# Winograd products with other signs, column sums from two blocks, and one block summed by transfers

## The chip, the core and the metric

The kernel runs on one core of a Trainium2 chip. The metric is the device time in microseconds of one execution.

## What is computed

```python
# for each of 128 samples b, x[b] is 64 x 1024
h     = gelu(gelu(cond @ W0 + b0) @ W1 + b1)
att   = softmax(h @ W2 + b2)                       # 128 x 8
agg_w = einsum('bk,koi->boi', att, weight)         # 64 x 64 for each sample
y     = agg_w[b] @ x[b] + (att @ bias_k)[b]        # mixes the 64 rows of a sample
logits, h = y @ W_router.T, y @ A.T                # 8 experts, rank 16, the top 2 of a softmax
out   = x + y @ W_base.T + b_base + 2 * (h * combine) @ B
```

All in fp32, 8192 rows of 1024 numbers.

## The kernel before

The two matmuls that take y's 1024 columns are one: A, W_router and W_base lie side by side in a matrix "wide" of 1024 x 1160 (128 columns for A, 8 for the router, 1024 for the base). Mixing a sample's rows and multiplying by "wide" commute, so the kernel first computes z = x @ wide, and then mixes: each pair of samples is a tile of 128 rows, multiplied by a block-diagonal 128 x 128 matrix ("mix", from agg_w). The bias agg_b of a row passes through "wide" as agg_b times the column sums of "wide"; these are computed once, by matmuls with a matrix of ones, into `col_sum` (lines 437 to 446).

**Splitting.** TensorE multiplies in fp32r. Each operand is a high part (a cast on ScalarE, `x_high`, `split_weight`) and a low part (the rest, by a subtraction on VectorE, `x_low`, `split_weight`, lines 912 and 1009). A product is high·high + high·low + low·high, three matmuls of 128 x 128 by 128 x 290 columns each (lines 416, 418, 420).

**Seven products.** Two tiles make a unit, 32 units in all. A unit's x is a 2 x 2 matrix of blocks (A11, A12 for the first tile, A21, A22 for the second; each 128 rows by 512), and "wide" is one too (B11, B12, B21, B22; each 512 x 580, split into 4 chunks of rows). From unit 1 on, Winograd's form of Strassen's scheme takes seven block products in place of eight; each is 24 matmuls. It needs sums of x's blocks (S1 to S4, made on VectorE for every unit, lines 915 to 928) and of the blocks of "wide" (T1 to T4, made once, line 1018, and split once, lines 722 and 1009). Unit 0 takes the plain eight products, while "wide" is still coming in; the T blocks are made beside it.

**What sets the order.** All five engines have their instructions written out by hand, in order, with semaphore waits. The stretch that matters is the end of unit 0 and unit 1. TensorE (lines 561 to 584): products A11·B12 and A12·B22 for Z12, the matmul that makes `agg_b` (line 567), the column sums of B11 and B21, the products A21·B12 and A22·B22 for Z22, with the column sums of B12 and of B22 between and after them, then mixing of tile 0 (`mixed`). The column sums and the matmul of agg_b use PSUM banks that the products and mixing use too: the A21·B12 product waits for VectorE's two copies of agg_b (line 1053), and a new set of column sums for ScalarE's copy of the last (line 733). ScalarE's order is in lines 776 to 796, VectorE's in lines 1041 to 1072, its unit 1 in lines 1074 to 1119. In unit 1 TensorE waits for the low parts of T2, T3 and T4 (lines 601, 610, 621), T1 being ready long before.

Staging: `w_stage` has two slots, B11's and B21's; T1, T2 and later T3 are made in B11's slot and T4 in B21's. B12 and B22 lie in `b12_sb` and `b22_sb`, whose bytes other buffers of the later work take over. `w_hi` and `w_lo` have six slots for seven blocks, B12's slot being given to another block after unit 0.

POOL makes the low part of "mix" (line 882) and adds x to the biases by an accumulating transfer (`add_x`, line 889): VectorE writes the biases into `x_sb` (`put_biases`, line 1002), the transfer adds x, and VectorE adds the result from PSUM (`result`, lines 995 and 997). SP issues all other loads and stores.

## Time and profile before

| | |
|---|---|
| median of 3 runs | 954.32 us (954.03 to 954.56) |
| the profiled execution | 954.3 us, its span 952.6 us |
| TensorE busy | 945.1 us, 99% of the span |
| VectorE, ScalarE, POOL busy | 695.5, 332.8, 89.1 us |
| share of the chain that ended last | TensorE 97%, DMA 1%, VectorE 1% |
| HBM | 75.37 MB read, 35.65 MB written, 117 GB/s over the span |

The span is the time from the first to the last instruction in the profile; the execution's own time is 1.7 us longer. Times in the timelines are from the start of the span. Matmuls are pipelined, so one that is printed as 0.30 us long starts 0.13 us after the one before it.

### The profile page before, as it was taken

Reading aid. Unit: us, or ns where it says so; the run is one execution under the profiler, and the core shown is the slowest. Engines: PE = TensorE matmul, PEld = TensorE weight load, DVE = VectorE, ACT = ScalarE, POOL = GpSimd, SP = SyncE. Lnnn points to the kernel's source line nnn. Section 1 sums busy time; section 2 is a strip of 40 time slices with the busy share of each in tenths; the row PEclk is TensorE's granted clock in tenths of the full one; section 3 lists DMA queues with packets and bytes.
Section 4 is the critical chain, followed back from the end, with each engine's and each line's share of the span. In section 5 each row is a group of like instructions: output and inputs, shape, how many; then the busy total and the mean of one; then the engine's idle time right before and its main releaser. Section 6 shows DMA issues by size and latency. Waiting matters only on the chain.

```text
span 952.6 us, 18810 instructions
## 1 busy us (share of the span) xinstructions
PE 945.1 (99%) x6745; PEld 940.2 (99%) x6745; DVE 695.5 (73%) x1554; ACT 332.8 (35%) x671; POOL 89.1 (9%) x134
## 2 busy tenths in 40 slices
PE   9999999999999999999999999999999999999997
PEld 8999999999999999999999999999999999999997
DVE  4889776768776768777777777777777677767686
ACT  5653332333332333332333333333333333323431
POOL 0011010101010100100100100010101010101010
...
GB/s 304 140 75 132 110 119 132 92 132 91 111 115 133 90 134 91 111 113 130 94 133 92 112 113 119 105 118 105 114 113 109 115 108 104 120 118 104 120 90 111
DMA packets 35233, 111.33 MB, mean 117 GB/s; under 512 B 13040, under 2 KB 13424, under 8 KB 30864
## 3 DMA queue, kind: packets, MB, share of 16 engines
...
q10 hardware_dynamic: 288, 1.19, 0.4%
...
q14 instruction: 6, 0.05, 0.0%
HBM read 75.37 MB, written 35.65 MB: 117 GB/s over the span
## 4 chain that ended last, share of the span: by engine, by line
PE 97%; DMA 1%; DVE 1%; issue 0%; ACT 0%; DVEq 0%; ACTq 0%
PE ps L416 25%; PE ps L420 25%; PE ps L418 25%; PE ps L476 9%; PE ps L452 4%; PE ps L450 4%; PE ps L454 4%; DMA w_stage<-in_wide 1%; PE ps L499 1%; PE ps L442 0%; PE ps L443 0%; PE ps L502 0%; PE ps L513 0%; DVE sum L931 0%; DVE x_sb L1220 0%
## 5 line engine op out<-in xcount | busy, mean ns | idle before, releaser
L416 PE MATMUL ps<-w_hi,x_hi 128*128 128x290 f32 x1544 | 460.3, 298 | 0.3 <-DVE sum L931 0.3
L418 PE MATMUL ps<-w_lo,x_hi 128*128 128x290 f32 x1544 | 457.7, 296 | 0.0
L420 PE MATMUL ps<-w_hi,x_lo 128*128 128x290 f32 x1544 | 456.9, 296 | 0.0
L416 PEld LDWEIGHTS ps<-w_hi,x_hi 128*128 128x128 f32 x1544 | 291.5, 189 | 2.5 <-issue 1.5
L420 PEld LDWEIGHTS ps<-w_hi,x_lo 128*128 128x128 f32 x1544 | 291.3, 189 | 0.0
L418 PEld LDWEIGHTS ps<-w_lo,x_hi 128*128 128x128 f32 x1544 | 291.2, 189 | 0.0
L684 ACT CAST x_hi<-xT_sb 128x512 fp32r<-128x512 f32 x186 | 115.6, 621 | 190.9 <-DVE xT_sb L928 163.4
L912 DVE TENSOR_TENSOR x_lo<-xT_sb,x_hi 128x512 fp32r<-128x512 f32 x186 | 127.4, 686 | 34.3 <-ACT x_hi L684 34.3
L889 POOL DMA_DIRECT2D x_sb<-in_x x64 | 56.4, 881 | 512.0 <-DVE x_sb L1002 512.0
L988 DVE TENSOR_TENSOR hwT_lo<-ps,hwT_hi 128x128 fp32r<-128x128 f32 x64 | 18.7, 291 | 97.7 <-ACT hwT_hi L696 96.9
L699 ACT COPY sum<-ps 128x580 f32<-128x580 f32 x96 | 61.9, 645 | 62.9 <-PE ps L420 62.1
L1002 DVE SCALAR_TENSOR_TENSOR x_sb<-col_sum,agg_b,bias_out 128x1024 f32<-128x1024 f32 x64 | 81.8, 1279 | 1.0 <-ACT col_sum L733 1.0
L931 DVE TENSOR_TENSOR sum<-ps,sum 128x580 f32<-128x580 f32 x92 | 69.6, 757 | 12.7 <-PE ps L420 12.6
L416 PE MATMUL ps<-t_hi,x_hi 128*128 128x290 f32 x248 | 76.4, 308 | 0.0
L420 PE MATMUL ps<-t_hi,x_lo 128*128 128x290 f32 x248 | 74.0, 298 | 0.0
L418 PE MATMUL ps<-t_lo,x_hi 128*128 128x290 f32 x248 | 73.4, 296 | 0.0
L707 ACT CAST z_hi<-sum 128x580 fp32r<-128x580 f32 x31 | 21.0, 678 | 148.8 <-DVE sum L931 148.8
L450 PE MATMUL ps<-z_hi,mix_hi 128*128 128x384 f32 x189 | 64.2, 339 | 0.7 <-DVE x_sb L997 0.7
L452 PE MATMUL ps<-z_hi,mix_lo 128*128 128x384 f32 x189 | 64.2, 340 | 0.0
L882 POOL TENSOR_TENSOR mix_lo<-mix,mix_hi 128x128 fp32r<-128x128 f32 x64 | 32.3, 506 | 340.1 <-ACT mix_hi L688 340.1
L454 PE MATMUL ps<-z_lo,mix_hi 128*128 128x384 f32 x189 | 63.5, 336 | 0.0
L997 DVE TENSOR_TENSOR x_sb<-ps,x_sb 128x776 f32<-128x776 f32 x62 | 59.2, 955 | 0.0
...
## 6 DMA issues: line engine op xcount, KB each, us to landing
x_sb<-in_x POOLq DMA_DIRECT2D x64, 512.0 KB, 5.4
result<-x_sb SPq DMA_DIRECT2D x63, 512.0 KB, 2.8
...
b_sb<-in_wide SPq DMA_DIRECT2D x2, 1160.0 KB, 14.7
agg_w_rows<-agg_w SPq DMA_DIRECT2D x1, 2048.0 KB, 7.5
...
```

What stands on the lines that cost most here:

```text
L416: nc.tensor.matmul(dst, x_hi[:, s, rows], high[:, c, cols], start=first, stop=False, skip_group_check=True)
L418: nc.tensor.matmul(dst, x_hi[:, s, rows], low[:, c, cols], start=False, stop=False, skip_group_check=True)
L420: mm = nc.tensor.matmul(dst, x_lo[:, s, rows], high[:, c, cols], start=False, stop=last, skip_group_check=True)
L450: nc.tensor.matmul(dst, mix_hi[:, side, :], high[:, columns(k)], start=start, stop=False, skip_group_check=True)
L452: nc.tensor.matmul(dst, mix_lo[:, side, :], high[:, columns(k)], start=False, stop=False, skip_group_check=True)
L454: return nc.tensor.matmul(dst, mix_hi[:, side, :], low[:, columns(k)], start=False, stop=True, skip_group_check=True)
L476: mm = nc.tensor.matmul(ps[:, banks[k], at], stat[:], mov[:, res], start=False, stop=True, skip_group_check=True)
L684: nc.scalar.copy(x_hi[:, SLOT[name], :], raw(name)).then_inc(x_hi_done, 1)
L699: nc.scalar.copy(dst[:], acc(first)).then_inc(done, 1)
L912: nc.vector.tensor_tensor(x_lo[:, SLOT[name], :], raw(name), x_hi[:, SLOT[name], :].bitcast(F32), ALU.subtract).then_inc(x_lo_done, 1)
L931: nc.vector.tensor_tensor(dst[:], acc(first), dst[:], ALU.add).then_inc(done, 1)
L1002: nc.vector.scalar_tensor_tensor(x_sb[:, side, :], col_sum[:, AR:WIDE], agg_b[:, bass.ds(tile_no(u, side), 1)], bias_out[:], ALU.mult, ALU.add
```

## The change

- The signs of S1, S2 and S3 are turned, and T1 to T4 follow: T1 = B12 - B11, T2 = T1 + B22, T3 = B12 + B22, T4 = B21 - T2. S1 goes with T1, S2 with T2, S3 with T3 and A22 with T4, as before.
- T3 + T4 = B11 + B21, and T3 is B12 + B22. So the column sums of T4 and of T3 suffice: T3's are the right half, and the left half is the sum of both, one more VectorE instruction. Two blocks are summed by TensorE instead of four.
- T3 is not made on VectorE: two accumulating transfers, issued by POOL, add B22 from HBM onto B12 in `b12_sb`.
- T4 and T3 are split in unit 0, T2 and T1 in unit 1 (before: T1 and T2 in unit 0, T3 and T4 in unit 1). T1 has the separate pair of buffers that T3 had.
- On VectorE, T1, T2 and T4 are made one after the other, ahead of the copies of agg_b. The low part of B goes from before the first biases into unit 1, and the biases of tile 1 go behind the low part of T1.
- SP loads the small table ahead of the rest of unit 0's x.

```diff
@@ -45,8 +45,9 @@
-B11, B21, T1, B22, T2, T4, T3 = range(7)
-B12 = T4
+B11, B21, T3, B22, T2, T4, T1 = range(7)
+B12 = T3
@@ -165,8 +166,8 @@
-        t3_hi = sb("t3_hi", [P, CHUNKS, HALF], F32R)
-        t3_lo = sb("t3_lo", [P, CHUNKS, HALF], F32R)
+        t1_hi = sb("t1_hi", [P, CHUNKS, HALF], F32R)
+        t1_lo = sb("t1_lo", [P, CHUNKS, HALF], F32R)
@@ -255,21 +258,22 @@
-        SPLIT_AT = {"B11": 4, "B21": 6, "B12": 7, "B22": 8, "T1": 9, "T2": 10, "T3": 11, "T4": 12}
+        SPLIT_AT = {"B11": 4, "B21": 6, "B12": 7, "B22": 8, "T4": 9, "T3": 10, "T2": 11, "T1": 12}
-        T_AT = {"T1": 1, "T2": 2, "T4": 3, "T3": 4}
+        T_AT = {"T1": 1, "T2": 2, "T4": 3}
-            return (t3_hi, t3_lo) if w == T3 else (w_hi[:, w, :, :], w_lo[:, w, :, :])
+            return (t1_hi, t1_lo) if w == T1 else (w_hi[:, w, :, :], w_lo[:, w, :, :])
-        b11_stage = t_stage = chunked(w_stage[:, 0, :])
+        b11_stage = t1_stage = chunked(w_stage[:, 0, :])
-        b12_stage = chunked(b12_sb[:])
-        b22_stage = chunked(b22_sb[:])
+        b12_stage = t3_stage = chunked(b12_sb[:])
+        b22_stage = t2_stage = chunked(b22_sb[:])
@@ -355,9 +359,9 @@
             sp.dma_start(xT_sb[:, 0, :], xT_units[0][:, 0:XBLOCK]).then_inc(first_xT_in[0], 16)
+            sp.dma_start(small_sb[:], small).then_inc(small_in, 16)
             sp.dma_start(xT_sb[:, 1:4, :].rearrange("p b n -> p (b n)"), xT_units[0][:, XBLOCK:]
-            sp.dma_start(small_sb[:], small).then_inc(small_in, 16)
@@ -434,16 +438,14 @@
                     mm = product_part(bank, name, part, start)
                 mm.then_inc(product_mm, 1)
-            def column_sums(bank, w, start=False, stop=False):
+            def column_sums(bank, w):
                 high, low = weight_parts(w)
                 for part in range(2):
                     dst, cols = ps[:, bank + part, 0:PART], slice(part * PART, (part + 1) * PART)
                     for c in range(CHUNKS):
-                        nc.tensor.matmul(dst, ones_r[:], high[:, c, cols], start=start and c == 0, stop=False)
-                        mm = nc.tensor.matmul(dst, ones_r[:], low[:, c, cols], start=False,
-                                              stop=stop and c == CHUNKS - 1)
-                if stop:
-                    mm.then_inc(col_mm, 1)
+                        nc.tensor.matmul(dst, ones_r[:], high[:, c, cols], start=c == 0, stop=False)
+                        mm = nc.tensor.matmul(dst, ones_r[:], low[:, c, cols], start=False, stop=c == CHUNKS - 1)
+                mm.then_inc(col_mm, 1)
             def mixed(side, k, bank=None, high=z_hi, low=z_lo, start=True):
                 dst = ps[:, O_BANK + k if bank is None else bank, 0:width(k)]
@@ -565,15 +567,15 @@
             first_product(b, "A12", B22, False)
             pe.wait_ge(agg_done, 2 * GROUPS)
             chain(ps[:, O_BANK, 0:BATCH], mix_w_sb[0:KERNELS, GROUP_COLS:MIX_COLS], attT[0:KERNELS, :], agg_b_mm)
-            pe.wait_ge(ones_done, 1)
-            column_sums(O_BANK + 2, B11, start=True)
-            column_sums(O_BANK + 2, B21, stop=True)
             pe.wait_ge(agg_b_done, 2)
             first_product(O_BANK, "A21", B12, True)
+            first_product(O_BANK, "A22", B22, False)
+            pe.wait_ge(ones_done, 1)
+            pe.wait_ge(w_lo_done, SPLIT_AT["T4"])
+            column_sums(O_BANK + 2, T4)
             pe.wait_ge(col_sum_done, 1)
-            column_sums(O_BANK + 2, B12, start=True)
-            first_product(O_BANK, "A22", B22, False)
-            column_sums(O_BANK + 2, B22, stop=True)
+            pe.wait_ge(w_lo_done, SPLIT_AT["T3"])
+            column_sums(O_BANK + 2, T3)
             pe.wait_ge(z22_summed, 1)
             pe.wait_ge(mix_lo_done, 1)
             pe.wait_ge(z11_lo_done, 1)
@@ -604,10 +606,10 @@
+                if first:
+                    pe.wait_ge(w_lo_done, SPLIT_AT["T1"])
-                if first:
-                    pe.wait_ge(w_lo_done, SPLIT_AT["T3"])
@@ -617,8 +619,6 @@
-                if first:
-                    pe.wait_ge(w_lo_done, SPLIT_AT["T4"])
@@ -776,24 +776,26 @@
             aggregated(0)
             z11_high(0)
             aggregated(1)
-            act.wait_ge(t_made, T_AT["T1"])
-            split_weight(T1, t_stage)
             act.wait_ge(product_mm, FIRST_PRODUCT["A12", B22])
             save(sum2, b, z12_summed)
             act.wait_ge(xT_in, 16)
             x_high("A11")
-            column_sum(0)
+            act.wait_ge(t_made, T_AT["T4"])
+            split_weight(T4, t4_stage)
+            z12_high(0)
             for side in range(2):
                 mix_high(0, side)
-            z12_high(0)
-            act.wait_ge(t_made, T_AT["T2"])
-            split_weight(T2, t_stage)
+            act.wait_ge(t3_in, 32)
+            act.wait_ge(product_mm, FIRST_PRODUCT["A21", B12])
+            split_weight(T3, t3_stage)
+            act.wait_ge(product_mm, FIRST_PRODUCT["A22", B22])
+            save(sum3, O_BANK, z22_summed)
             x_high("A12")
+            column_sum(0)
+            split_weight(T2, t2_stage)
+            column_sum(1)
             act.wait_ge(bT_in, 16)
             nc.scalar.copy(b_hi[:], bT_stage).then_inc(b_hi_done, 1)
-            act.wait_ge(product_mm, FIRST_PRODUCT["A22", B22])
-            save(sum3, O_BANK, z22_summed)
-            column_sum(1)
             def unit(u, par, first=False):
                 a, b = accumulators(par)
@@ -809,8 +811,8 @@
-                    act.wait_ge(t_made, T_AT["T3"])
-                    split_weight(T3, t_stage)
+                    act.wait_ge(w_lo_done, SPLIT_AT["T3"])
+                    split_weight(T1, t1_stage)
@@ -819,8 +821,6 @@
-                if first:
-                    split_weight(T4, t4_stage)
@@ -888,6 +888,13 @@
                 pool.wait_ge(biased, t + 1)
                 pool.dma_start(x_sb[:, side, :], x_tiles[t], accum_op=ALU.add).then_inc(x_in[side], 16)
+
+            pool.wait_ge(b12_in, 16)
+            pool.wait_ge(w_lo_done, SPLIT_AT["B12"])
+            pool.wait_ge(t_made, T_AT["T1"])
+            for js in HALVES:
+                cols = slice(js.start * HALF, js.stop * HALF)
+                pool.dma_start(b12_sb[:, cols], wide_blocks[3][:, cols], accum_op=ALU.add).then_inc(t3_in, 16)
             for side in range(2):
                 mix_low(0, side)
             add_x(0, 0)
@@ -913,15 +920,15 @@
-                nc.vector.tensor_tensor(raw("S1"), raw("A21"), raw("A22"), ALU.add).then_inc(s_made, 1)
+                nc.vector.tensor_tensor(raw("S1"), raw("A21"), raw("A22"), ALU.subtract).then_inc(s_made, 1)
-                nc.vector.tensor_tensor(raw("S3"), raw("A11"), raw("A21"), ALU.subtract).then_inc(s_made, 1)
+                nc.vector.tensor_tensor(raw("S3"), raw("A21"), raw("A11"), ALU.subtract).then_inc(s_made, 1)
-                nc.vector.tensor_tensor(raw("S2"), raw("S1"), raw("A11"), ALU.subtract).then_inc(s_made, 1)
+                nc.vector.tensor_tensor(raw("S2"), raw("A11"), raw("S1"), ALU.subtract).then_inc(s_made, 1)
@@ -1014,8 +1021,8 @@
                 nc.vector.tensor_tensor(x_lo[:, FIRST_SLOT[name], :], xT_sb[:, RAW[name], :],
                                         x_hi[:, FIRST_SLOT[name], :].bitcast(F32), ALU.subtract).then_inc(x_lo_done, 1)
-            def make_t(dst, left, right):
-                nc.vector.tensor_tensor(dst, left, right, ALU.subtract).then_inc(t_made, 1)
+            def make_t(dst, left, right, op=ALU.subtract):
+                nc.vector.tensor_tensor(dst, left, right, op).then_inc(t_made, 1)
             nc.vector.memset(att[:], 0.0).then_inc(att_step, 1)
             first_x_low("A11")
@@ -1041,34 +1048,34 @@
             split_weight(B12, SPLIT_AT["B12"], b12_stage)
             split_weight(B22, SPLIT_AT["B22"], b22_stage)
             dve.wait_ge(w_lo_done, SPLIT_AT["B11"])
-            make_t(t_stage, b12_stage, b11_stage)
+            make_t(t1_stage, b12_stage, b11_stage)
+            dve.wait_ge(w_lo_done, SPLIT_AT["B22"])
+            dve.wait_ge(t_made, T_AT["T1"])
+            make_t(t2_stage, t1_stage, b22_stage, ALU.add)
+            dve.wait_ge(t_made, T_AT["T2"])
+            make_t(t4_stage, b2_stage, t2_stage)
             z11_low(0)
-            dve.wait_ge(xT_in, 16)
-            make_s1(1)
-            make_s3(1)
             dve.wait_ge(agg_b_mm, 1)
             for par in range(PAIR):
                 rows = slice(par * CH, (par + 1) * CH)
                 of_tiles = ps[rows, O_BANK, 0:BATCH].rearrange("p (t par) -> p t par", par=PAIR)[:, :, par]
                 nc.vector.tensor_copy(agg_b[rows, :], of_tiles).then_inc(agg_b_done, 1)
-            split_weight(T1, SPLIT_AT["T1"], t_stage)
+            dve.wait_ge(xT_in, 16)
+            make_s1(1)
+            make_s3(1)
+            split_weight(T4, SPLIT_AT["T4"], t4_stage)
+            split_weight(T3, SPLIT_AT["T3"], t3_stage)
+            z12_low(0)
             x_low(1, "A11")
-            dve.wait_ge(w_lo_done, SPLIT_AT["T1"])
-            dve.wait_ge(t_made, T_AT["T1"])
-            make_t(t_stage, b22_stage, t_stage)
-            z12_low(0)
-            dve.wait_ge(t_made, T_AT["T2"])
-            make_t(t4_stage, b2_stage, t_stage)
-            split_weight(T2, SPLIT_AT["T2"], t_stage)
             x_low(1, "A12")
             dve.wait_ge(x_lo_done, splits(1, "A11"))
             make_s2(1)
-            dve.wait_ge(b_hi_done, 1)
-            nc.vector.tensor_tensor(b_lo[:], bT_stage, b_hi[:].bitcast(F32), ALU.subtract).then_inc(b_lo_done, 1)
+            dve.wait_ge(col_sum_done, 2)
+            nc.vector.tensor_tensor(col_sum[:, 0:HALF], col_sum[:, 0:HALF], col_sum[:, HALF:WIDE], ALU.add
+                                    ).then_inc(col_left_done, 1)
             dve.wait_ge(bias_out_in, 16)
             dve.wait_ge(agg_w_out, 16)
-            dve.wait_ge(col_sum_done, 2)
-            dve.wait_ge(b_lo_done, 1)
+            dve.wait_ge(col_left_done, 1)
             put_biases(0, 0)
             def unit_1():
@@ -1077,21 +1084,23 @@
                 z21_low(0, b)
                 route(0, 0)
                 x_low(1, "S2")
+                dve.wait_ge(b_hi_done, 1)
+                nc.vector.tensor_tensor(b_lo[:], bT_stage, b_hi[:].bitcast(F32), ALU.subtract).then_inc(b_lo_done, 1)
+                hwT_low(0, 0)
+                split_weight(T2, SPLIT_AT["T2"], t2_stage)
                 z22_low(0)
-                hwT_low(0, 0)
-                x_low(1, "S1")
-                put_biases(0, 1)
-                dve.wait_ge(w_lo_done, SPLIT_AT["T2"])
-                dve.wait_ge(t_made, T_AT["T4"])
-                make_t(t_stage, b22_stage, b12_stage)
                 dve.wait_ge(p1_saved, 1)
                 dve.wait_ge(product_mm, products(1, "A12"))
                 add_acc(sum1, b, z11_summed)
                 result(0, 0)
+                x_low(1, "S1")
+                dve.wait_ge(w_lo_done, SPLIT_AT["T2"])
+                split_weight(T1, SPLIT_AT["T1"], t1_stage)
+                dve.wait_ge(b_lo_done, 1)
+                put_biases(0, 1)
                 x_low(1, "S3")
                 dve.wait_ge(x_lo_done, splits(1, "A12"))
                 make_s4(1)
-                split_weight(T3, SPLIT_AT["T3"], t_stage)
                 route(0, 1)
                 x_low(1, "S4")
                 x_low(1, "A22")
@@ -1100,7 +1109,6 @@
-                split_weight(T4, SPLIT_AT["T4"], t4_stage)
```

VectorE at the end of unit 0: the rows after the low parts of B12 and B22, before (`w_stage` holds T1, then T2 and T4; `b_sb` is b12_sb or b22_sb).

```order
L1018 TENSOR_TENSOR w_stage<-b_sb,w_stage 128x2320 [waits w_lo_done]
L935 TENSOR_TENSOR z_lo<-sum,z_hi 128x580 [waits z11_hi_done]
L916 TENSOR_TENSOR s_sb<-xT_sb 128x512 [waits xT_in]
L920 TENSOR_TENSOR xT_sb<-xT_sb 128x512 [waits s_made]
L1053 COPY agg_b<-ps 64x64 [waits agg_b_mm]
L1053 COPY agg_b<-ps 64x64
L1009 TENSOR_TENSOR w_lo<-w_stage,w_hi 128x2320 [waits w_hi_done]
```

The same place with the change.

```order
L1025 TENSOR_TENSOR w_stage<-b_sb,w_stage 128x2320 [waits w_lo_done]
L1025 TENSOR_TENSOR b_sb<-w_stage,b_sb 128x2320 [waits t_made,w_lo_done]
L1025 TENSOR_TENSOR w_stage<-w_stage,b_sb 128x2320 [waits t_made]
L942 TENSOR_TENSOR z_lo<-sum,z_hi 128x580 [waits z11_hi_done]
L1062 COPY agg_b<-ps 64x64 [waits agg_b_mm]
L1062 COPY agg_b<-ps 64x64
L923 TENSOR_TENSOR s_sb<-xT_sb 128x512 [waits xT_in]
L927 TENSOR_TENSOR xT_sb<-xT_sb 128x512 [waits s_made]
L1016 TENSOR_TENSOR w_lo<-w_stage,w_hi 128x2320 [waits w_hi_done]
L1016 TENSOR_TENSOR w_lo<-b_sb,w_hi 128x2320 [waits w_hi_done]
```

Three makes of a T stand ahead of the two copies of agg_b, where one stood; the two sums of x's blocks went behind them.

TensorE at the matmul of agg_b, before (the two rows ahead of it end A12·B22; the rows behind it begin the column sums).

```order
L418 MATMUL ps<-w_lo,x_hi 128x290
L420 MATMUL ps<-w_hi,x_lo 128x290
L502 MATMUL ps<-attT,mix_w_sb 128x128 [waits agg_done]
L442 MATMUL ps<-w_hi,ones_r 128x290 [waits ones_done]
L443 MATMUL ps<-w_lo,ones_r 128x290
```

The same place with the change.

```order
L422 MATMUL ps<-w_lo,x_hi 128x290
L424 MATMUL ps<-w_hi,x_lo 128x290
L504 MATMUL ps<-attT,mix_w_sb 128x128 [waits agg_done]
L420 MATMUL ps<-w_hi,x_hi 128x290 [waits agg_b_done]
L422 MATMUL ps<-w_lo,x_hi 128x290
```

The product that waits for the copies of agg_b comes right behind the matmul that makes it.

VectorE in unit 1, from the first low part of an S block to the make of S4, with the change.

```order
L919 TENSOR_TENSOR x_lo<-xT_sb,x_hi 128x512 [waits x_hi_done]
L1088 TENSOR_TENSOR b_lo<-x_sb,b_hi 128x1024 [waits b_hi_done]
L995 TENSOR_TENSOR hwT_lo<-ps,hwT_hi 128x128 [waits hwT_hi_done]
L1016 TENSOR_TENSOR w_lo<-b_sb,w_hi 128x2320 [waits w_hi_done]
L957 TENSOR_TENSOR z_lo<-sum,z_hi 128x580 [waits z22_hi_done]
L938 TENSOR_TENSOR sum<-ps,sum 128x580 [waits product_mm,p1_saved]
L1002 TENSOR_TENSOR x_sb<-ps,x_sb 128x248 [waits out_mm,x_in_a]
L1004 TENSOR_TENSOR x_sb<-ps,x_sb 128x776
L919 TENSOR_TENSOR x_lo<-s_sb,x_hi 128x512 [waits x_hi_done]
L1016 TENSOR_TENSOR t_lo<-w_stage,t_hi 128x2320 [waits w_hi_done,w_lo_done]
L1009 SCALAR_TENSOR_TENSOR x_sb<-col_sum,agg_b,bias_out 128x1024 [waits b_lo_done]
```

Two splits of a T (rows L1016, of T2 and T1) and b_lo now stand between the low part of S2 and the biases of tile 1, where the make of T3 stood alone.

## Rows read from the trace of the kernel before

**Rows 1.** The page, busy time of the engines
```profile
PE 945.1 (99%) x6745; PEld 940.2 (99%) x6745; DVE 695.5 (73%) x1554; ACT 332.8 (35%) x671; POOL 89.1 (9%) x134
```

**Rows 2.** TensorE's waits, whole span: who waited for whom, total, times, longest, us
```profile
PE ps L513 <- ACT w_hi L722: 0.9, 1, 0.9
```

**Rows 3.** TensorE's timeline: start us, duration us, engine, line, operation, tiles
```profile
33.73 0.40 PE L442 MATMUL ps<-w_hi,ones_r 128*128 128x290 f32 x1
33.97 0.30 PE L443 MATMUL ps<-w_lo,ones_r 128*128 128x290 f32 x1
...
38.01 0.30 PE L443 MATMUL ps<-w_lo,ones_r 128*128 128x290 f32 x1
...
48.86 0.33 PE L450 MATMUL ps<-z_hi,mix_hi 128*128 128x384 f32 x1
```

**Rows 4.** VectorE's timeline, end of unit 0
```profile
25.21 2.58 DVE L1009 TENSOR_TENSOR w_lo<-b_sb,w_hi 128x2320 fp32r<-128x2320 f32 x1 [0.82 <-ACT w_hi L722]
27.70 2.57 DVE L1018 TENSOR_TENSOR w_stage<-b_sb,w_stage 128x2320 f32<-128x2320 f32 x1
30.19 0.76 DVE L935 TENSOR_TENSOR z_lo<-sum,z_hi 128x580 fp32r<-128x580 f32 x1
...
33.84 0.48 DVE L1053 COPY agg_b<-ps 64x64 f32<-64x64 f32 x2 [1.57 <-PE ps L502]
```

**Rows 5.** SP's and ScalarE's timelines, and the landing times of b12_sb and b22_sb
```profile
6.36 0.45 SPq L369 DMA_DIRECT2D b_sb<-in_wide  x1
...
23.04 2.14 ACT L722 CAST w_hi<-b_sb 128x2320 fp32r<-128x2320 f32 x1
...
38.34 0.65 ACT L733 COPY col_sum<-ps 128x580 f32<-128x580 f32 x1 [3.19 <-PE ps L443]
...
DMA to landing us min/median/max: 12.7/14.7/16.6
```

**Rows 6.** Timelines of VectorE, ScalarE and TensorE, 47 to 65 us
```profile
47.69 1.22 DVE L1067 TENSOR_TENSOR b_lo<-x_sb,b_hi 128x1024 fp32r<-128x1024 f32 x1 [0.30 <-ACT b_hi L793]
49.91 1.28 DVE L1002 SCALAR_TENSOR_TENSOR x_sb<-col_sum,agg_b,bias_out 128x1024 f32<-128x1024 f32 x1 [1.00 <-ACT col_sum L733]
51.32 0.76 DVE L945 TENSOR_TENSOR z_lo<-ps,z_hi 128x580 fp32r<-128x580 f32 x1
...
53.87 0.68 DVE L912 TENSOR_TENSOR x_lo<-xT_sb,x_hi 128x512 fp32r<-128x512 f32 x1
...
61.35 0.95 DVE L997 TENSOR_TENSOR x_sb<-ps,x_sb 128x776 f32<-128x776 f32 x1
...
64.06 0.64 ACT L699 COPY sum<-ps 128x580 f32<-128x580 f32 x1
...
58.39 0.30 PE L416 MATMUL ps<-w_hi,x_hi 128*128 128x290 f32 x1
...
62.45 0.41 PE L450 MATMUL ps<-z_hi,mix_hi 128*128 128x384 f32 x1 [0.68 <-DVE x_sb L997]
...
64.11 0.29 PE L416 MATMUL ps<-w_hi,x_hi 128*128 128x290 f32 x1
```

**Rows 7.** DMA: 83 to 89 us; issues of 125 to 140 us, then whole span
```profile
83.00:89.00 6.00, 5.97 (x44) 5.74 (x43) 5.20 (x19) 1.72 (x5) 1.22 (x2) 1.00 1.00 178
...
x_sb<-in_x POOLq DMA_DIRECT2D x1, 512.0 KB, 5.4
result<-x_sb SPq DMA_DIRECT2D x1, 512.0 KB, 5.3
...
result<-x_sb SPq DMA_DIRECT2D x63, 512.0 KB, 2.8
agg_w_rows<-agg_w SPq DMA_DIRECT2D x1, 2048.0 KB, 7.5
```

**Rows 8.** Warm-up matmuls by stretch: us, busy and (count) for matmul, then load, clock, DMA
```profile
4.00:7.00 3.00, 3.00 (x16) 3.00 (x15) 1.00 0.94 323
7.00:8.50 1.50, 1.50 (x15) 1.50 (x13) 1.00 0.98 407
```

2 lines of the change are left out of this document (added).

## The prediction

> **What bounds the kernel now.** I read the page's busy line first, then TensorE's waits, then the timelines of TensorE, VectorE and ScalarE from 20 to 80 us, and last the transfers. TensorE is busy in 945.1 of 952.6 us [rows 1]; its waits are few, and the largest after its first matmul is 0.9 us, for a cast of B11 [rows 2]. So a matmul taken out of TensorE's stream is time taken out of the span, if everything TensorE then waits for is ready earlier by as much. The reader is to see in the timelines that, after the first loads, VectorE is nearly as full as TensorE up to 80 us: it makes and splits the seven weight blocks there. The profiled execution took 954.3 us beside a median of 954.32, so I add to 954.3.
>
> A rule of reading that I use throughout: on VectorE an operation starts about 0.09 us before the printed end of the one before it, if it does not depend on it (25.21 to 27.70 is 2.49 for a row of 2.58 [rows 4]). One that needs the other's result starts about 0.04 us after it.
>
> **1. Column sums, removed.** Before, B11, B21, B12 and B22 are summed, 16 matmuls each. Now T4 and T3 alone: 32 fewer. The spacing is (38.01 - 33.97) / 30 = 0.1347 us [rows 3]. 32 x 0.1347 = **-4.31 us**, all on TensorE's path.
>
> **2. agg_b, a new wait.** The column sums of B11 and B21 stood between the matmul that makes agg_b (it ends at about 33.8) and the product A21·B12, which writes the same PSUM bank and so must wait for VectorE's two copies of agg_b. Those sums ran from 33.73 to 38.1 [rows 3] and the copies at 33.84 to 34.32 [rows 4]: hidden. Now the product comes at once, and on VectorE three makes of a T (T1, T2, T4) stand ahead of the copies instead of one. Worked out from rows 4: T1 27.70 to 30.27; T2 needs T1, 30.31 to 32.88; T4 needs T2, 32.92 to 35.49; the low part of Z11 starts at 35.41, and the copies at 36.08, ending at 36.56. TensorE goes on at about 36.66 instead of 33.73: **+2.93 us**. Queued behind this wait are both remaining products of unit 0, both column sums and all of unit 1. The start of the chain is fixed by a transfer: B22 lands at 6.36 + 16.6 = 22.96, its cast starts at 23.04 [rows 5], its low part at 25.21. The wait could be 0.2 either side of this.
>
> **3. T4's sums to T3's sums, a new wait.** Both use one pair of banks. Before, a product lay between a pair of sums and the next. Now T3's sums wait for ScalarE's copy of T4's. From rows 3 and 5: the last sum of a pair started at 38.01, the copy ran from 38.34 to 38.99, so TensorE can go on at 39.04, where it would have at 38.14: **+0.90 us**, and 0.10 for one more restart (the first matmul after a wait takes 0.24 instead of 0.13, 33.73 to 33.97 [rows 3]).
>
> So the first mixing matmul of unit 0, at 48.86 before [rows 3], comes 4.31 - 2.93 - 0.90 - 0.10 = **0.38 us earlier**, at 48.48. The second copy of column sums is then at 48.7 to 49.35, with the cast of T2 done on ScalarE before it.
>
> **4. T3 by transfers.** POOL waits for T1 (30.27) and issues two accumulating transfers of 580 KB at about 30.6. Two of 512 KB kept the engines full for 6 us at 178 GB/s [rows 7]; 1.19 MB at that rate is 6.7 us, starting 1.5 us after the issue: landed at about 39.3. ScalarE may not cast T3 before A21·B12 has been multiplied (w_hi's slot), at about 40.2, and TensorE needs T3's low part at 46.3, which allows the cast to start as late as 41.5 (2.14 + 2.57 + small change). So the transfer is hidden, with 2.2 us in hand; I take **0**. What shares the engines is the 2,048 KB store of agg_w from 35.3 on [rows 7]. Beside an add, a store of 512 KB took 5.3 us instead of 2.8, while the add kept its 5.4 [rows 7]: the store pays, and nobody waits for agg_w before 49. Bounds: 0, and +2 if the two queues shared evenly (below). The Trainium skill's page "DMA: Bandwidth & Descriptors", section "Queues, rings and completion order", says that an engine goes round-robin between the queues it has work for, a packet at a time; by that T3 would be slowed as well, and the sum would be up to 2 us higher. The rows speak for the add keeping its pace.
>
> **5. Unit 1, where VectorE sets the pace.** VectorE now adds the two halves' sums first (580 columns, 0.76) and then makes the first biases: 49.55 + 0.76 + 0.04 = 50.35, instead of 49.91 [rows 6]. From there to the low part of S2 it took 3.96, of which 0.22 was a wait before Z21 (51.32) that is over now: 54.09. Then low S2 0.60, b_lo 1.13, hwT_lo 0.21, and the low part of T2 from 56.05 to **58.61**. TensorE wants T2 at 58.39 - 0.38 = 58.01 [rows 6]: it waits 0.70 with the latency of 0.1. Low Z22 0.67, Z11's sum 0.67, result 1.20 (before, this result was what mixing waited for, 0.68 [rows 6]; now it is out at 61.2, in time), low S1 0.60, and T1's low part ends at **64.24**. TensorE, from 58.71: S2 24 x 0.1347 + 0.1 to 62.04, mixing 1.60 to 63.64, then T1: another 0.70, to 64.34. Biases 1.20, low S3 0.60, S4 made by 66.65; ScalarE casts it and then saves U2, done at **67.86** instead of 64.70 [rows 6]; TensorE, ready at 67.67, starts S3 at 67.91. Before, it started S3 at 64.11 + 3.23 = 67.34 [rows 6]. So unit 1 turns the lead of 0.38 into a lag of 0.57, with the restart **0.67 us**. Bounds for this part: each of those three instants may be off by 0.3.
>
> **6. The rest.** From unit 2 on a subtraction stands where an addition stood, of the same size and place: 0. No T is split late in unit 1 any more (two splits and a make fewer there, one split and b_lo more), so nothing is carried into unit 2. The table "small" is loaded ahead of 768 KB of x: B11's second half may land sooner, which is worth 0 to 0.9 us at TensorE's wait [rows 2]. But whatever is gained is lost at step 2, because there TensorE waits for a chain that hangs on B22's landing, whose place in the queue has not moved: 0 in the sum, and a wait of up to 3.8 us instead of 2.9.
>
> **Sum:** -4.31 + 2.93 + 0.90 + 0.10 + 1.05 (unit 1: from -0.38 to +0.67) = +0.67. Forecast **955.0 us**, no change: about 1.9 us (0.2%) is what a measurement can tell.
>
> **Rivals.** (a) *The clock falls in the new gap: slower.* Since its first matmul TensorE has never stood still for more than 0.9 us [rows 2]. After standing idle, the warm-up passed 16 matmuls in 3 us from 4 to 7, and 15 in 1.5 us from 7 to 8.5, at a clock column of 1.00 in both [rows 8]: a half-speed stretch of some 5.9 us (1.1 to 7.0) that the column does not show. If an idle gap of 2.9 to 3.8 us brings that back, at the lower of the two levels (1.2 and 2.4 GHz), TensorE loses half of up to 5.9 us: +1.7 to +2.9, giving 956.7 to 957.9. It decides from the point at which the gap is long enough, and the trace has none to tell. The Trainium skill, "TensorE: Matmul & The Clock Gate", Part 1, has the throttled state as the default to which an idle engine returns; by that rule this is the case, if the gap is long enough. Chance 0.25. (b) *T3 lands late: slower.* If from 36 us both queues get half, the last 2.8 us of T3 take 5.6 or, with the store's larger pieces, 7.4: 41.7 to 43.4, so 0.2 to 1.9 after the limit of 41.5: up to 956.9. Against it: rows 7. Chance 0.08. (c) *The wait at agg_b is short and unit 1 does not wait: faster.* Then only 0.9 is given back: 954.3 - 4.3 + 1.0 = 951.0. It would need the three makes to take 3.2 us less; rows 4 give 2.57 each. Chance 0.05. (d) *The start's 0.9 us counts after all,* as B22 lands sooner too: 954.1. Chance 0.07, and still no change.
>
> **How the numbers follow.** The forecast itself 0.55, at 954.2 to 956.0. Faster by over 0.2% only by (c), with room for something not seen: 0.07. Slower by over 0.2% (over 956.2): (a), and half of (b), 0.28. No change: 0.65. The range goes from (d) to (a): 953.6 to 958.0.
>
> **What would show it.** Right: TensorE waits about 2.9 us (up to 3.8) before its first product after the agg_b matmul, released by VectorE's copy; 0.9 us between the two runs of column sums, released by ScalarE; 0.7 us each before S2 and S1 in unit 1, released by splits; and no wait in mixing at 62. Wrong: the copies of agg_b at 34 us; T3's cast starting later than 41.5; matmuls 0.25 us apart after the gap; or unit 2 starting at another lag than 0.67.

## The result, and the profile after

| | before | changed |
|---|---|---|
| median, in the same session | 954.4 us (12 runs, 954.03 to 954.77) | 956.85 us (12 runs, 956.49 to 957.41) |
| the profiled execution, its span | 954.3, 952.6 us | 956.55, 954.7 us |
| mean granted clock over the span | 1.000 | 0.998 |

The ratio is 1.0025, with an interval of 1.0018 to 1.0033: the changed kernel is 2.4 us slower. That lies inside the predicted range (953.6 to 958.0), but the forecast itself, 955.0 and no change, was 1.85 us too low, and it was the wrong case: slower by more than 0.2%, to which the prediction had given 0.28.

The page, busy time of the engines, of the changed kernel:

```profile
PE 942.5 (99%) x6713; PEld 936.8 (98%) x6713; DVE 693.7 (73%) x1554; ACT 332.3 (35%) x671; POOL 88.1 (9%) x136
```

Against [rows 1] there are 32 matmuls fewer, as the diff says. At the 0.1347 us of step 1 the busy time should be 4.3 us less, and it is 2.6 less. So there is more than new waits: some matmuls became longer. The waits of TensorE, in the columns of [rows 2]:

```profile
PE ps L420 <- DVE agg_b L1062: 3.3, 1, 3.3
...
PE ps L446 <- DVE w_lo L1016: 1.1, 1, 1.1
PE ps L420 <- DVE t_lo L1016: 0.6, 1, 0.6
PE ps L420 <- issue: 0.6, 1, 0.6
...
PE ps L515 <- ACT w_hi L722: 0.3, 1, 0.3
```

The first is the predicted wait for agg_b. The second was predicted as a wait for ScalarE's copy of the column sums, but it is VectorE's split of T3 that ends it. The next two are T1 and T2 in unit 1 (that of T2 is put down to "issue"). The last was 0.9 in [rows 2]. TensorE's timeline gives the places (start, duration, then what ended the idle time before it):

```profile
32.44 0.48 PE L504 MATMUL ps<-attT,mix_w_sb 8*128 8x128 f32 x2
...
36.21 0.40 PE L420 MATMUL ps<-w_hi,x_hi 128*128 128x290 f32 x1 [3.29 <-DVE agg_b L1062]
...
44.24 0.29 PE L446 MATMUL ps<-w_hi,ones_r 128*128 128x290 f32 x1
...
46.24 0.29 PE L447 MATMUL ps<-w_lo,ones_r 128*128 128x290 f32 x1
47.59 0.38 PE L446 MATMUL ps<-w_hi,ones_r 128*128 128x290 f32 x1 [1.06 <-DVE w_lo L1016]
...
60.14 0.37 PE L420 MATMUL ps<-w_hi,x_hi 128*128 128x290 f32 x1 [0.59 <-issue]
...
65.81 0.37 PE L420 MATMUL ps<-t_hi,x_hi 128*128 128x290 f32 x1 [0.64 <-DVE t_lo L1016]
...
69.31 0.40 PE L420 MATMUL ps<-w_hi,x_hi 128*128 128x290 f32 x1
```

Between 36.21 and 44.24 there are 48 matmuls. At the usual spacing they take 6.5 us, and they took 8.03. The stretches of 1 us (the stretch, its length, busy time and number of instructions of PE, PEld, DVE, ACT and POOL) show why (the last three columns are the granted clock, the DMA share and GB/s):

```profile
36.00:37.00 1.00, 0.79 (x5) 0.80 (x6) 0.94 (x3) 1.00 (x1) 0.00 (x0) 0.93 0.91 146
37.00:38.00 1.00, 1.00 (x6) 1.00 (x5) 1.00 (x2) 0.83 (x2) 0.00 (x0) 0.50 0.97 175
38.00:39.00 1.00, 1.00 (x6) 1.00 (x6) 1.00 (x1) 0.00 (x0) 0.00 (x0) 0.50 0.99 192
39.00:40.00 1.00, 1.00 (x6) 1.00 (x6) 1.00 (x1) 0.00 (x0) 0.00 (x0) 0.50 0.48 96
40.00:41.00 1.00, 1.00 (x8) 1.00 (x8) 0.09 (x1) 0.00 (x0) 0.00 (x0) 0.86 0.37 32
41.00:42.00 1.00, 1.00 (x10) 1.00 (x9) 0.00 (x0) 0.00 (x0) 0.00 (x0) 1.00 1.21 499
```

TensorE stood for 3.29 us and started again at 36.21, and from 36.9 (0.93 is a mean over the stretch) to 40.3 the granted clock was 0.50, the 1.2 GHz level: 3.4 us. This is rival (a). ScalarE's and VectorE's timelines show that T3 was late as well, as in rival (b):

```profile
42.12 0.69 ACT L688 CAST mix_hi<-mix 128x128 fp32r<-128x128 f32 x2 [4.29 <-DMA mix<-agg_w]
42.71 2.13 ACT L722 CAST w_hi<-b_sb 128x2320 fp32r<-128x2320 f32 x1
...
44.87 2.58 DVE L1016 TENSOR_TENSOR w_lo<-b_sb,w_hi 128x2320 fp32r<-128x2320 f32 x1 [4.79 <-ACT w_hi L722]
```

The cast of T3 began at 42.71, not at 40.2, and later than the limit of 41.5 that step 4 gives. And the transfers behind it (issue, landing; first SyncE's, then by group):

```profile
31.27 7.54 SPq L351 DMA_DIRECT2D mix<-agg_w  x4
...
b_sb<-in_wide POOLq DMA_DIRECT2D x2, 580.0 KB, 9.5
...
mix<-agg_w SPq DMA_DIRECT2D x4, 16.0 KB, 8.0
```

T3's two halves took 8.3 and 10.8 us instead of the 8.2 of step 4 (1.5 and 6.7), so that the second landed at 42.1. The four loads of 16 KB for the first two mixing matrices took 8.0 to land, and 7.54 to be issued. In the profile before, the same four were issued at 32.15 in 3.08 us and landed in 2.7.

The twelve executions are not all like the profiled one. Seven have a mean clock of 0.998 over the span and a median of 956.70 us; five have 0.995 or 0.996 and a median of 957.09. What a lower mean clock looks like is shown by the profiles of runs 3, 5 and 9 below.

So there are two suspects, and they stand in parallel: the clock makes A21·B12 and A22·B22 end 1.5 us late, and T3's low part, wanted right behind them, is late too. The experiments had to part them.

### The profile page after: what moved, and what is told of

The parts are those of the page before. It is cut to its first block, busy times and chain, and to the rows that moved or that the text cites. A ratio compares the mean times of both kernels' runs of the same rounds, so it can differ in the third digit from the quotient of the medians.

```text
span 954.7 us, 18751 instructions
## 1 busy us (share of the span) xinstructions
PE 942.5 (99%) x6713; PEld 936.8 (98%) x6713; DVE 693.7 (73%) x1554; ACT 332.3 (35%) x671; POOL 88.1 (9%) x136
## 3 DMA queue, kind: packets, MB, share of 16 engines
q10 hardware_dynamic: 288, 1.19, 0.4%
## 4 chain that ended last, share of the span: by engine, by line
PE 95%; DVE 2%; DMA 2%; ACT 1%; SPq 0%; issue 0%; DVEq 0%; ACTq 0%
PE ps L420 25%; PE ps L424 24%; PE ps L422 24%; PE ps L478 9%; PE ps L454 3%; PE ps L452 3%; PE ps L456 3%; DMA w_stage<-in_wide 1%; DMA mix<-agg_w 1%; PE ps L501 1%; SPq L351 0%; ACT w_hi L722 0%; PE ps L504 0%; DVE w_lo L1016 0%; DVE t_lo L1016 0%
## 5 line engine op out<-in xcount | busy, mean ns | idle before, releaser
L420 PE MATMUL ps<-t_hi,x_hi 128*128 128x290 f32 x248 | 73.7, 297 | 0.6 <-DVE t_lo L1016 0.6
L882 POOL TENSOR_TENSOR mix_lo<-mix,mix_hi 128x128 fp32r<-128x128 f32 x64 | 29.7, 465 | 308.3 <-ACT mix_hi L688 308.3
```

The source lines that it names most:

```text
L420: nc.tensor.matmul(dst, x_hi[:, s, rows], high[:, c, cols], start=first, stop=False, skip_group_check=True)
```

## Experiments

Times are medians, with the kernel before run beside them on the same chip: 954.36 for runs 1 to 4, 954.44 for runs 5 to 7 and 11, 954.37 for runs 8 to 10 and 12. The rows of a run come from one execution, the profiled one.

**1. The gap taken away.**

```diff
+            (the two copies of agg_b)
             dve.wait_ge(t_made, T_AT["T2"])
             make_t(t4_stage, b2_stage, t2_stage)
...
-            (the two copies of agg_b)
```

> The copies of agg_b ahead of T4's make on VectorE. Theory M (what sets the time is T3's low part, at 47.4 us, because ScalarE's cast of T3 stands behind the casts of mix, whose loads land 8.0 us after their issue beside the transfers that add B22): TensorE waits 0.6 instead of 3.3 us for agg_b, the clock does not fall, and TensorE then waits about 2.5 us longer for T3's low part; the time stays within 0.3 us of the change's 956.85. Theory C (the wait for agg_b and the fallen clock are on the path): 2.7 + 1.6 us less, minus some 0.7 that T4 is later: 953.3.

Measured: 958.62 us, ratio 1.0045 (1.0031 to 1.0059), slower than the changed kernel. A row of TensorE's timeline and one stretch, in its last three columns the granted clock, the DMA share and GB/s:

```profile
47.89 0.58 PE L446 MATMUL ps<-w_hi,ones_r 128*128 128x290 f32 x1 [4.57 <-DVE w_lo L1016]
...
48.00:49.00 1.00, 1.00 (x5) 1.00 (x6) 1.00 (x3) 0.76 (x1) 0.00 (x0) 0.50 0.47 70
```

The gap at agg_b shrank to 0.57 and the clock stayed at 1.00 behind it. T4's sums started at 40.93. But T3's sums could not start before 47.89: the same gap, with the same fall of the clock behind it, now fell between the two runs of column sums. Here T3 sets the end of unit 0, not agg_b. Theory M had the waits right, but the time lies 1.8 us over its 956.85: it had no fall of the clock behind the second gap.

**2. T3 cast before the mixing matrices.**

```diff
             act.wait_ge(t3_in, 32)
-            for side in range(2):
-                mix_high(0, side)
             split_weight(T3, t3_stage)
+            for side in range(2):
+                mix_high(0, side)
```

> ScalarE casts T3 ahead of the two casts of mix. Theory M with C (both end at nearly the same instant): T3's cast starts at 40.9, when A21*B12 is through, its low part ends at 45.7, and TensorE is now held by the copy of T4's sums, at 47.26 instead of 47.59: 956.5. Theory M alone (the clock's fall costs nothing anywhere): T3 1.8 us sooner gives up to 1.8 us: 955.1.

Measured: 956.83 us, 1.0024 (1.0015 to 1.0033), as the changed kernel.

```profile
42.14 2.13 ACT L722 CAST w_hi<-b_sb 128x2320 fp32r<-128x2320 f32 x1 [4.17 <-DMA b_sb<-in_wide]
...
47.41 0.40 PE L446 MATMUL ps<-w_hi,ones_r 128*128 128x290 f32 x1 [0.73 <-ACT col_sum L733]
```

The order on ScalarE was not the cause: now the transfer itself ends the wait, at 42.14, and only 0.57 of lateness goes. T3's sums then wait for ScalarE's copy, 0.18 sooner than before, and the time does not move, since the clock fell in the gap as before. Together with run 4 below: either cause alone is enough for almost all of the delay.

**3. Both edits.** 

> Both edits: copies of agg_b ahead of T4's make, and T3's cast ahead of the casts of mix. Theory M with C: no long gap, no fall of the clock; TensorE waits 0.7 for T4's low part and starts T3's sums at about 45.1 instead of 47.59, 2.5 us less: 954.4, though either edit alone gives at most 0.3. If the two costs simply add: the sum of the gains of the two edits alone.

Measured: 957.94 us, 1.0035 (1.0021 to 1.0048). T3's sums waited 4.09 us for the low part, and the clock was at 0.50 from 46 to 52. The forecast of 954.4 missed: T3 landed no sooner than before, its cast could start only at 42.53, and the gap was run 1's again. This fall lasted 6.8 us, from 45.8 to 52.7.

**4. The gap filled.** 24 matmuls of the ones, into a free bank, between the matmul of agg_b and its wait.

```diff
+            pe.wait_ge(ones_done, 1)
+            for _ in range(24):
+                nc.tensor.matmul(ps[:, T_BANK, 0:PART], ones_r[:], w_hi[:, B11, 0, 0:PART], start=True, stop=True)
             pe.wait_ge(agg_b_done, 2)
```

> 24 matmuls of 290 columns on a spare PSUM bank, of no use to the result, in the gap before A21*B12: TensorE is busy while it waits for agg_b. The clock should stay at 1.00. Theory M: TensorE reaches T3's sums 1.6 us sooner and waits as much longer for T3's low part: 956.8. Theory C: the fall of the clock is on the path: 955.2.

Measured: 957.83 us (956.20 to 958.14), 1.0030 (1.0018 to 1.0041). The products then took 6.5 us at full clock and the last of T4's sums started at 44.98. But T3's sums waited 2.70 for the low part, until 47.97, and in the profiled execution the clock fell behind that gap. Four of the seven executions took 957.8 to 958.1 at a mean clock of 0.998, the other three 956.2 to 956.8 at 1.000. So with the clock full all along, T3's lateness by itself still gives 956.5, close to theory M's 956.8.

**5 to 7. Without the transfers.** In these three T3 stands for B12 alone: the addition of B22 is left out, and the result lacks it.

```diff
-            act.wait_ge(t3_in, 32)
...
-                pool.dma_start(b12_sb[:, cols], wide_blocks[3][:, cols], accum_op=ALU.add).then_inc(t3_in, 16)
```

Run 5 has this edit alone. 

> The two transfers that add B22 onto B12 are left out, so T3 stands for B12 alone. Theory T (the runs before this leave it: T3's transfers land at about 42 us, 11.5 after their issue, and delay SP's four loads of mix from 2.7 to 8 us; T3's low part, at 47.4, sets the time wherever TensorE's gap lies): the loads of mix land in 3 us again, T3's cast starts when A21*B12 is through (40.9 with the fallen clock), and TensorE starts T3's sums at about 47.2, held by the copy of T4's: 956.5. Rival (the transfers are not the cause, the casts' place is): no change in the loads' landing, T3's low part still at 47.4, 956.8.

Run 6 has the filling matmuls too. 

> As the last, with the 24 filling matmuls in the gap. Here nothing late hides the clock: theory T has its fall cost 1.6 us, so this should be 1.3 to 1.6 us faster than without the filling: 955.1. If the clock's fall costs nothing: the same as without the filling.

Run 7 has, in place of them, the copies of agg_b ahead of T4's make. 

> No transfers (T3 stands for B12), and the copies of agg_b ahead of T4's make. Theory T: both holds are gone; TensorE goes on at 33.5, waits 0.8 for T4's low part and about 0.9 for the copy of its sums, starts T3's sums at 44.1 instead of 47.6, and later waits in unit 1 as before: 3.4 us less than the change, 953.4. If something else holds T3's sums at 47.5, the time stays at 957 or above.

| run | edit | us | ratio, interval | A21·B12, T3's sums start |
|---|---|---|---|---|
| 5 | no addition | 956.22 (954.43 to 957.38) | 1.0016 (1.0007 to 1.0025) | 36.21, 48.48 |
| 6 | and the gap filled | 954.95 (954.51 to 955.08) | 1.0004 (0.9995 to 1.0013) | 36.38, 45.92 |
| 7 | and the copies first | 953.14 (952.71 to 953.48) | 0.9986 (0.9977 to 0.9995) | 33.49, 44.15 |

The last column is of the profiled executions, and run 5's was the slowest of its eleven, 957.38 us: its clock was at 0.50 from 35.4 to 42.2, 6.8 us and not 3.4, so its 48.48 is later than in most. Taking the transfers away alone brings only 0.6 us, since the clock still falls in the gap. Run 6 against run 5 is the price of the clock in the medians: 1.27 us. One execution of run 5 had a mean clock of 1.000 and took 954.43; eight with 0.997 or 0.998 took 955.8 to 956.4, which is 1.2 us above run 6 in the median, and two with 0.995, as profiled, took 957.0 and 957.4, 2.0 and 2.4 above it. Run 7 against run 6 is the price of the waiting itself: 1.81 us. With no transfer in the way, removing the wait at agg_b pays that much; with it (run 1), it costs 1.8. And the small loads land in 2.3 us here, issued in 2.5: it was the accumulating transfers that slowed them.

**8. T1 made first.** The transfers wait for T1 to have read B12. Here VectorE makes T1 before B22's low part.

```diff
-            split_weight(B22, SPLIT_AT["B22"], b22_stage)
             make_t(t1_stage, b12_stage, b11_stage)
+            split_weight(B22, SPLIT_AT["B22"], b22_stage)
```

> One edit to the changed kernel: T1 is made ahead of B22's low part on VectorE, so the transfers of T3 (which wait for T1 to have read B12) are issued some 3.5 us sooner, at about 27. The chain that ends at agg_b's copies keeps its length: it moves by nothing or by the 0.4 that VectorE waited for B22's cast. T3 sets the restart: the transfers land at 34 to 38, T3's sums no longer wait for a split (the 1.06 goes), the gap before A21·B12 is 2.5 to 3.3, and the clock falls there as before. Time 955.2 to 955.9, at a gap of 3.3. If the gap shrinks to 2.1 and the clock holds, 954.0. If T3's transfers had no part in it: 956.8.

Measured: 955.38 us (953.56 to 955.65), 1.0004 (0.9995 to 1.0013). The transfers were issued at 27.04, and the slower half took 8.1; T3's sums waited for the copy alone:

```profile
45.22 0.29 PE L447 MATMUL ps<-w_lo,ones_r 128*128 128x290 f32 x1
46.24 0.40 PE L446 MATMUL ps<-w_hi,ones_r 128*128 128x290 f32 x1 [0.73 <-ACT col_sum L733]
```

The gap at agg_b was 2.01 us. Behind it the clock fell in the profiled execution, for 3.4 us. Seven of eleven executions had a mean clock of 0.997 or 0.998 and took 955.37 to 955.65; the other four had 1.000 and took 953.56 to 954.04. The same kernel so gives the price of one such fall with nothing else changed, from the two medians: 955.49 - 953.89 = 1.60 us.

**9. The start undone.** The small table behind x again, as before the change.

```diff
-            sp.dma_start(small_sb[:], small).then_inc(small_in, 16)
             sp.dma_start(xT_sb[:, 1:4, :] ...
+            sp.dma_start(small_sb[:], small).then_inc(small_in, 16)
```

> One edit to the changed kernel: the table small is loaded behind x again. Forecast: TensorE's wait for B11's second half is back (0.9 instead of 0.3), and B22's cast, with it the whole chain to agg_b's copies, starts 0.4 later (23.0 instead of 22.6), so that the first mixing matmul comes 0.4 later: 957.2. If the reorder at the start is worth nothing, 956.8; if all of the 0.9 counts, 957.7.

Measured: 957.91 us (956.90 to 959.02), 1.0036 (1.0022 to 1.0049). A21·B12 started at 36.65, where the changed kernel has 36.21 and step 2 has 36.66. So the reorder brings this point forward by 0.44. It does so through B22's cast, not through TensorE's wait for B11's second half, 0.9 in [rows 2]: run 5's profile has that wait at 1.1 in all, the changed kernel's at 0.3, and both restart at 36.21. The medians differ by 1.1, but these executions scatter over 2.1 us, so no finer price is read from them. The profiled one, 958.96 us at a mean clock of 0.995, shows where a part of the scatter lies: its clock fell twice, for 3.4 us each, from 36.4 behind the gap of 2.88 and from 50.1, behind a gap of 1.86 before T3's sums at 48.73.

**10. What holds T3 up.** As run 2, and SyncE issues the small loads and all behind them only when T3 is in.

```diff
+            sp.wait_ge(t3_in, 32)
             load_first_mix(0)
             load_first_mix(1)
```

> The kernel with T3's cast ahead of the casts of the first mixing matrices (run before: T3 landed at 42.1, 11.5 after its issue, and the cast began at 42.14), with one more edit: SyncE issues the four small loads of the first mixing matrices, and the store of agg_w and what follows, only when T3 is in. If the small loads (or SyncE's other transfers) hold T3 up, it lands at 38 to 39.5, its cast begins at about 40.5, when A21·B12 has been multiplied, the wait before T3's sums is ScalarE's copy's (0.7), and the small loads take 2.7 again. If T3 takes 11.5 by itself, its cast begins at 42.1 as before, and TensorE then waits longer for the mixing matrices. Time: 956.3 by the first, 958 to 960 by the second.

Measured: 958.75 us, 1.0047 (1.0034 to 1.0061); the first sentence held for the transfers. Their halves landed in 5.8 and 8.4 us, so T3 was in at 39.7 instead of 42.1, and SyncE's timeline has the small loads right behind it:

```profile
39.74 2.50 SPq L351 DMA_DIRECT2D mix<-agg_w  x4
```

They landed in 2.3. T3's cast began at 41.38, released by TensorE, and its sums waited only for the copy. The time did not fall as that theory had it (956.3), since all that was held back on SyncE came late: TensorE waited 1.32 for a low part in mixing, and 1.05 ahead of S2.

What of the 2.4 us is the small loads', and what the store's, is read from the bytes moved up to 38.8, when the changed kernel's store of agg_w is issued. First run 10, then run 2, in the columns used above:

```profile
30.00:38.80 8.80, 5.62 (x35) 5.26 (x34) 8.67 (x8) 5.23 (x7) 1.91 (x2) 0.90 0.75 136
38.80:42.20 3.40, 3.40 (x21) 3.40 (x21) 1.37 (x1) 0.82 (x1) 0.00 (x0) 0.77 0.13 11
```

```profile
30.00:38.80 8.80, 5.43 (x34) 5.08 (x33) 8.62 (x8) 5.11 (x7) 1.91 (x2) 0.90 0.73 124
38.80:42.20 3.40, 3.40 (x22) 3.40 (x21) 1.43 (x1) 0.06 (x1) 0.00 (x0) 0.76 0.68 203
```

Run 10 had moved 8.8 x 136 = 1.20 MB by then, which is all of T3 (1.19 MB). The two queues apart, in packets (the pieces that the DMA engines move) and MB, first POOL's, which is T3, then SyncE's:

| stretch | run 10 | run 2 | changed kernel |
|---|---|---|---|
| 30.0 to 38.8 | 283, 1.18; none | 244, 1.06; 139, 0.03 | 248, 1.07; 146, 0.03 |
| 38.8 to 40.5 | 5, 0.00; none | 40, 0.12; 124, 0.03 | 37, 0.11; 125, 0.03 |
| 40.5 to 41.2 | none; 27, 0.01 | 2, 0.01; 46, 0.01 | 1, 0.00; 37, 0.01 |
| 41.2 to 42.2 | none; 121, 0.02 | 2, 0.00; 42, 0.51 | 2, 0.00; 43, 0.51 |

From 36.0 to 38.8 the changed kernel's two queues passed 104 and 105 packets, one for one, though T3's are of 4.6 KB and the small loads' of under 512 bytes. So the small loads took turns and hardly any bytes, and at 38.8 T3 was 0.11 to 0.12 MB behind run 10: at 178 GB/s 0.6 to 0.7 us of the 2.4. The store took no part in that, nor in most of what followed: issued at 38.86, it moved its first 0.5 MB only from 41.2 on, when two packets of T3 were left. The other 1.7 us are a tail. After 40.5 only three or four packets of T3 were left, some 0.01 MB, and they took until 42.1 to land, though the DMA share was 0.37 from 40 to 41. It stands in all six profiles in which the small loads were issued behind the transfers and beside them (runs 1 to 4, 9, the changed kernel): T3's slower half took 10.8 to 11.5 us there, and 8.0 to 8.4 in runs 8 and 10 to 12. What holds the last packets up, no run shows; no run holds back the small loads or the store alone. In run 9 SyncE issued the store at 35.28, the DMA engines moved 293 GB/s from 40 to 41 (32 in the changed kernel), and T3 landed at 43.1, so there the store may have had a part.

**11. A new order of the making.** T1 first; then B22's low part, T2, the copies of agg_b, T4; T2's cast and low part in unit 0 already; T3's cast before the mixing matrices'.

```diff
+            make_t(t1_stage, b12_stage, b11_stage)
             split_weight(B22, SPLIT_AT["B22"], b22_stage)
-            make_t(t1_stage, b12_stage, b11_stage)
             make_t(t2_stage, t1_stage, b22_stage, ALU.add)
+            (low part of Z11, S1 and S3 of unit 1, the two copies of agg_b)
             make_t(t4_stage, b2_stage, t2_stage)
-            (low part of Z11, the two copies of agg_b, S1 and S3 of unit 1)
+            split_weight(T2, SPLIT_AT["T2"], t2_stage)
             split_weight(T4, SPLIT_AT["T4"], t4_stage)
             split_weight(T3, SPLIT_AT["T3"], t3_stage)
```

> A version meant to keep the gain: T1 is made ahead of B22's low part (VectorE idles there), so the transfers start at 26.3 instead of 30.5 and are mostly done before SP's loads of mix; the copies of agg_b ahead of T4's make; T2 cast behind the agg_w copies and its low part made in unit 0, in VectorE's idle time before T4's low part; T3's cast ahead of those of mix. Theory T: no wait for T3, none for T2 and T1 in unit 1: mixing starts at 46.4 instead of 48.9 before, and its wait of 0.7 in unit 1 is gone: 951.2. Rival (unit 1's VectorE work or late transfers hold it all the same): 954 or above.

Measured: **952.19 us** (951.98 to 952.73), 0.9977 (0.9968 to 0.9986): faster than the kernel before by 2.2 us and than the changed one by 4.7. TensorE's waits:

```profile
PE ps L446 <- DVE w_lo L1017: 1.0, 1, 1.0
PE ps L420 <- DVE agg_b L1064: 0.8, 1, 0.8
PE ps L446 <- ACT col_sum L733: 0.7, 1, 0.7
```

No gap behind agg_b's matmul is over 1.0, the granted clock is 1.00 in every stretch from 33 to 51, the transfers land in 5.7 and 8.0, and of unit 1's two waits for splits none is left. T3's sums start at 44.55 instead of 47.59. The time is 1.0 above the forecast of 951.2, and well under the rival's 954. The run changes four things at once, and it does not tell what each brings.

**12. Fewer waits still, with GpSimd's help.** As run 11; agg_b's matmul and T3's sums go to banks that nobody holds, T4 is made right behind T2, and GpSimd makes S1 and S3 of unit 1 and the low part of b.

```diff
-            chain(ps[:, O_BANK, 0:BATCH], ..., agg_b_mm)
-            pe.wait_ge(agg_b_done, 2)
+            chain(ps[:, T_BANK, 0:BATCH], ..., agg_b_mm)
...
-            column_sums(O_BANK + 2, T3)
+            column_sums(b, T3)
...
+            nc.gpsimd.tensor_tensor(raw("S1"), raw("A21"), raw("A22"), ALU.subtract).then_inc(s_made, 1)
```

> The kernel with the new order of the making (run before) with three further edits: agg_b's matmul goes to a bank that no product of this stretch writes, so that A21·B12 waits for no copy, and ScalarE copies agg_b; T3's sums go to the banks of T1's and T2's products, so that they don't wait for the copy of T4's sums; two differences of unit 1 and the low part of b go to GpSimd. Forecast: no wait before A21·B12 (0.8 less), none of 0.9 before T4's sums and 0.1 instead of 0.7 before T3's, so 2.3 less at most; 949.3 to 950.5. Rival: VectorE, full until 44, is the bound, T4's and T3's low parts come no sooner, and the time stays at 952.2; or GpSimd's work slows VectorE and it is slower.

Measured: 953.63 us (952.46 to 954.64), 0.9994 (0.9985 to 1.0003): 1.4 slower than run 11. The rival held. Both waits for copies are gone, and T4's sums started only 0.21 sooner, since VectorE's low part of T4 was wanted by then. VectorE's and GpSimd's timelines show the rest:

```profile
28.64 3.90 DVE L1037 TENSOR_TENSOR b_sb<-w_stage,b_sb 128x2320 f32<-128x2320 f32 x1
32.57 3.54 DVE L1037 TENSOR_TENSOR w_stage<-w_stage,b_sb 128x2320 f32<-128x2320 f32 x1
...
30.17 3.50 POOL L907 TENSOR_TENSOR xT_sb<-xT_sb 128x512 f32<-128x512 f32 x1
```

The makes of T2 and T4 took 3.90 and 3.54 us beside GpSimd's two subtractions (28.1 to 33.7), where the same makes take 2.57 [rows 4]. VectorE lost 2.3 us to be spared 1.4 (two of 0.69). The run shows only that they overlap and that VectorE is slower where they do. The profiled execution, 952.46 us, is the fastest of eleven and only 0.4 above run 11's, so most of the 1.4 between the medians stands in no row. The Trainium skill, "Advanced Engine Details and Errata", section "Mode Summary", says that VectorE's second port to SBUF is shared with GpSimd, so that GpSimd's instructions and VectorE's two-port ones block each other. Its table gives an operation on two tensors, as these makes are, no two-port mode; the trace has them slowed all the same, and no run shows whether the port is the cause.

## Why the prediction was right or wrong

**Step 1, column sums, right.** T4's 16 sums run from 44.24 to 46.24, 0.133 us apart; 32 fewer are 4.3 us.

**Step 2, agg_b, right, and a part of it in rival (d).** It said a wait of 2.93 (up to 3.8) and a restart at 36.66; the profile has 3.29 and 36.21. Run 9 separates the two: with the start as before, it is 2.88 and 36.65. Step 6 said that the reorder at the start is worth nothing at this point, because B22's place in the queue had not moved. B22's cast nevertheless began at 22.58 instead of 23.04, and the restart came 0.45 sooner.

**Step 3, right in its size.** Run 8, where T3 is in time, has 1.02 from the last sum to the next pair's first, against 1.03.

**Step 4, T3's transfers hidden: this is the step that failed.** It took 6.7 us at full rate and a start after 1.5, named the store of agg_w as all that shares the engines, and put the term at 0. Alone, the transfers do land at 39.7 (run 10), 0.4 from the estimate. Beside SyncE's transfers T3 landed at 42.1, and its cast began at 42.71, with the limit at 41.5. What stood beside it was not the store, whose bytes moved from 41.2 on, but the four small loads, of which the prediction had no word: 0.6 to 0.7 us went to their turns, and 1.7 us are the tail of the last packets, whose cause stays open. Rival (b) named a landing between 41.7 and 43.4, and 42.1 lies inside, but it got there by the store taking half the rate from 36 on, which did not happen: the number was luck. The reading of [rows 7], that an add keeps its pace beside a store, was not tested by the changed kernel. The Trainium skill, "DMA: Bandwidth & Descriptors", section "Queues, rings and completion order", has an engine going round-robin between its queues, a packet at a time; the trace agrees, with 104 packets against 105, and it is the turns of many small packets that the prediction should have priced.

**Rival (a), the clock, the second term put at nothing.** It was given 0.25, and it came in all twelve executions of the changed kernel (mean clock 0.995 to 0.998). The forecast for it was a loss of 1.7 to 2.9 us, the lower bound worked out from no row; a fall of 3.4 us cost 1.60 (run 8) or 1.2 (run 5), and the two executions of run 5 at 0.995, one with a fall of 6.8 us in its profile, lost 2.0 and 2.4. The warm-up [rows 8] had suggested up to 5.9 at half speed. The Trainium skill, "TensorE: Matmul & The Clock Gate", Part 1, has an idle engine return to its slow state; the stretches above agree.

With both out of the way, the rest of the sum holds: run 6 took 954.95, and run 5's one execution at full clock 954.43, where the forecast was 955.0 and the restart came up to 0.45 sooner than in it.

**Step 5, unit 1, right.** The rows of the kernel before to hold against 69.31 and against the 74.23 at which the changed kernel starts S4:

```profile
67.31 0.29 PE L416 MATMUL ps<-t_hi,x_hi 128*128 128x290 f32 x1
...
72.07 0.29 PE L416 MATMUL ps<-w_hi,x_hi 128*128 128x290 f32 x1
```

The lag went from 0.96 at the first mixing matmul (49.82 against 48.86) to 2.00 at S3 and 2.16 at S4, which is 1.20 where 1.05 was predicted. The waits were 0.59 and 0.64 instead of 0.70 each, mixing at 63.4 did not wait, and U2's copy ended at 69.27, just ahead of S3.

**The sum, again.** At the first mixing matmul: predicted -0.38; the restart 0.45 sooner; the clock +1.51 (48 matmuls in 8.03 instead of 6.52); T3 beyond the copy +0.32. That makes +1.00, measured 0.96. With unit 1's 1.20 it is 2.16, and the profiled executions differ by 2.25. The clock and T3 don't add: in the changed kernel T3 would have held TensorE until nearly the same time had the clock been full (run 4, 47.97), and the clock alone with T3 in time gives nearly the same as well (run 2, 47.41). That is why each single repair measured as nothing or worse, and of the kernels that leave nothing out only those with the order that mends both (run 11, and 12 by less) are below the kernel before.
